# Three mixes in a row: a new order of TensorE's step in a one-core Metaformer kernel, with other banks for the projection and both layers

## The reference

```python
x = x + conv_ref(ln_over_channels(x), w_pc, w_in, fft_w, w_out)
t = to_tokens(x)
t = t + ffn(ln(t), W1, b1, W2, b2)        # products of fp8 (5,2) values, sums kept as fp16
x = from_tokens(t)

def conv_ref(x, w_pc, w_in, fft_w, w_out):
    x = concat([conv3x3(x[:, :12], w_pc), x[:, 12:]])
    x = conv1x1(x, w_in)                  # 48 -> 254 channels
    x = irfft2(rfft2(patches_8x8(x)) * fft_w)
    a, b = split(x, 2)                    # 127 channels each
    return conv1x1(gelu(a) * b, w_out)    # 127 -> 48
```

## Time and profile before

| what | us |
|---|---|
| median of 3 runs (691.2 to 693.7) | 692.02 |
| the profiled execution | 691.75 |
| its span, from the first to the last instruction | 689.9 |
| PE busy | 663.6 |
| DVE busy | 595.6 |
| ACT busy | 534.6 |
| POOL busy | 458.3 |

### The profile page before, as it was taken

One profiled execution on the slowest core, in us unless ns is written; L12 is line 12 of the kernel. 1 busy time (PEld: TensorE's weight loads), 2 busy tenths in 40 slices (PEclk: granted clock), 3 DMA queues, 4 the chain that ended last, 5 costly groups with the idle time before them and its releaser, 6 DMA issues.

```text
span 689.9 us, 19144 instructions
## 1 busy us (share of the span) xinstructions
PE 663.6 (96%) x6604; PEld 525.4 (76%) x6604; DVE 595.6 (86%) x1159; ACT 534.6 (77%) x1086; POOL 458.3 (66%) x348
## 2 busy tenths in 40 slices
PE   6789999999999999999999999999999999999984
PEld 5567787887778878777878787778778877787751
DVE  6668898899988988999889889998988899877887
ACT  3234588988888889888888888888888888777784
POOL 4535667687777777876777778767777787753353
PEclk9999999999999999999999999999999999999995
DMA  4544444554445545544454455445544554342102
GB/s 102 99 112 123 122 103 115 146 141 125 119 118 135 136 114 136 140 128 108 122 141 127 114 143 139 124 107 124 145 118 125 141 141 111 99 123 74 44 24 69
DMA packets 52207, 80.73 MB, mean 117 GB/s; under 512 B 20823, under 2 KB 36079, under 8 KB 52111
## 3 DMA queue, kind: packets, MB, share of 16 engines
q1 hardware_dynamic: 49823, 78.30, 44.2%
q10 hardware_dynamic: 2288, 1.20, 0.7%
HBM read 63.17 MB, written 16.30 MB: 115 GB/s over the span
## 4 chain that ended last, share of the span: by engine, by line
PE 88%; DVE 3%; issue 2%; POOL 2%; DMA 1%; ACT 1%; SPq 1%; DVEq 0%; POOLq 0%; ACTq 0%
PE inva L542 18%; PE invb L549 16%; PE mixp L529 13%; PE misc L558 8%; PE misc L819 8%; PE misc L629 4%; PE misc L529 4%; PE misc L673 3%; PE misc L778 3%; PE misc L578 3%; PE misc L587 2%; PE misc L663 2%; PE mixp L642 2%; PE mixp L649 2%; POOL st L1596 1%
## 5 line engine op out<-in xcount | busy, mean ns | idle before, releaser
L1596 POOL TENSOR_TENSOR st<-st,neg_half 128x16 f32<-128x16 f32 x32 | 92.8, 2901 | 118.6 <-DVE st L1502 118.5
L542 PEld LDWEIGHTS inva<-inv,gmix 128*127 128x127 f32 x1024 | 123.3, 190 | 24.9 <-DVE gmix L1274 12.8
L542 PE MATMUL inva<-inv,gmix 128*127 128x128 f32 x1024 | 141.0, 280 | 0.2 <-DVE gmix L1274 0.2
L1274 DVE TENSOR_TENSOR gmix<-mixp,freq_w 128x508 f32<-128x508 f32 x192 | 122.5, 679 | 15.9 <-PE mixp L529 15.9
L549 PE MATMUL invb<-inv,gmix 128*127 128x128 f32 x1024 | 134.7, 274 | 0.1
L549 PEld LDWEIGHTS invb<-inv,gmix 128*127 128x127 f32 x1024 | 126.1, 191 | 2.1 <-DVE hbuf L1285 0.5
L912 ACT ACTIVATE hid<-misc 128x512 f16<-128x512 f32 x180 | 93.9, 595 | 17.6 <-PE misc L629 17.6
L1630 POOL TENSOR_TENSOR st<-st,neg_half 128x16 f32<-128x16 f32 x31 | 95.5, 3080 | 16.3 <-DVE st L1353 16.3
L1285 DVE TENSOR_TENSOR hbuf<-gact,invb 127x512 f32<-127x512 f32 x128 | 87.3, 682 | 21.3 <-ACT gact L904 16.7
L904 ACT ACTIVATE gact<-inva 127x512 f32<-127x512 f32 x128 | 77.1, 603 | 21.8 <-PE inva L542 21.2
L921 ACT ACTIVATE hid<-hid 128x512 fp8e5<-128x512 f16 x174 | 93.2, 618 | 0.0
(11 more groups left out here) (187 smaller groups left out, 1332.6 us busy)
## 6 DMA issues: line engine op xcount, KB each, us to landing
taps<-cz_scratch SPq DMA_DIRECT2D x63, 292.2 KB
xres<-in_x_dram SPq DMA_DIRECT2D x64, 192.0 KB, 4.3
xin<-in_x_dram SPq DMA_DIRECT2D x63, 192.0 KB, 3.4
out_dram<-ob SPq DMA_DIRECT2D x60, 192.0 KB, 2.6
taps<-cz_scratch SPq DMA_DIRECT2D x63, 146.1 KB
crm<-rm_scratch SPq DMA_DIRECT2D x58, 96.0 KB
cx<-in_x_dram SPq DMA_DIRECT2D x32, 96.0 KB
cz_scratch<-cz SPq DMA_DIRECT2D x63, 48.8 KB
```

The costliest lines, as they stand in the source:

```text
L542: mm = pe.matmul(inva[0:HID, q * PX:(q + 1) * PX], gmix[:, s % 2, q, 0:HID], inv[:], start=True, stop=True, skip_group_check=True)
L1274: dve.tensor_tensor(gmix[:, s % 2, 2 * q:2 * q + 2, 0:HID2], pair[q][:, 0:2 * HID2].rearrange("p (e c) -> p e c", e=2), freq_w[:], ALU.mul ...
L1596: pool.tensor_tensor(st1[:, 6, :], st1[:, 5, :], neg_half[:], ALU.pow).then_inc(pow1, 1)
```

## The change

Mix 2 is written directly behind mixes 0 and 1 and goes to `misc2` and `misc3`; mix 1 stays in `misc0` and `misc1`, mixes 0 and 3 in the `mixp` banks. `gmix` has four slots, so weighing s waits for the inverse s of the band before. The projection goes to the `mixp` banks (before: `misc3` and `misc2`), the second layer to `misc0` and `misc1` (before: `mixp`). The first layer's order is now (0,2), then behind the stream the pair (0,0) and (0,1), mix 3, (1,0), (1,1), `convolve`, and (1,2), written (c,g); each has its bank in a table. From band 3 on the stream uses `misc1` (before: `misc3`). ACT's copies of the first layer follow that order, the last of them in the next step; `order_x` stands ahead of the second layer's copies (`sums`). On DVE weighing 0 stands ahead of the gate 3 of the band before, weighing 2 and gate 0 ahead of the second layer's bias. On SP `rows_in` stands ahead of the store of the output.

The diff, cut to its core:

```diff
-        gmix = sb("gmix", [128, 2, 4, 256])
+        gmix = sb("gmix", [128, 4, 4, 256])
...
+        mix_pair = (mixp, bank[0:2], bank[2:4], mixp)
+        def stream_bank(c):
+            return bank[3 if c < 3 else 1]
+        MADE = {(0, 2): 1, (0, 0): 2, (0, 1): 3, (1, 0): 4, (1, 1): 5, (1, 2): 6}
+        RELUED = {(0, 2): 1, (0, 0): 3, (0, 1): 3, (1, 0): 5, (1, 1): 5, (1, 2): 6}
+        hid_bank = {(0, 2): bank[0], (0, 0): bank[3], (0, 1): bank[2],
+                    (1, 0): bank[0], (1, 1): bank[3], (1, 2): bank[2]}
... (PE, mix and second_layer)
-                pe.wait_ge(gmix_ready, upto(8 * n + 2 * (s if s != 1 else 0)))
-                pair = bank if s == 1 else mixp
+                if s == 0:
+                    pe.wait_ge(gmix_ready, upto(8 * n))
+                pair = mix_pair[s]
...
-                pair = mixp
-                pe.wait_ge(gmix_ready, upto(8 * n + 2, 8 * STEPS))
+                pair = bank
                 pe.wait_ge(hid8_ready, upto(6 * l + 5))
                 pe.sem_inc(pe_held, 1)
                 for c in range(2):
+                    pe.wait_ge(gmix_ready, upto(8 * n + 3 + c, 8 * STEPS))
... (PE, step)
                     mix(t, 1)
+                    pe.wait_ge(hid16_ready, upto(6 * l + 6))
+                    mix(t, 2)
                 if live(t, 4):
-                    pe.wait_ge(lo_ready, upto(2 * n + 1, 2 * STEPS))
-                    project(t, 0, bank[3])
-                    pe.wait_ge(hid16_ready, upto(6 * l + 6))
-                    project(t, 1, bank[2])
+                    pe.wait_ge(gmix_ready, upto(8 * n + 1))
+                    project(t, 0, mixp[0])
+                    pe.wait_ge(gmix_ready, upto(8 * n + 2))
+                    project(t, 1, mixp[1])
...
-                if live(t, 3):
-                    pe.wait_ge(y16_ready, upto(2 * l + 2))
-                    if a >= ROWS_EARLY:
-                        pe.wait_ge(rmT_ready, upto(a + 1, STEPS))
-                    mix(t, 2)
-                if live(t, 5):
-                    pe.wait_ge(q16_ready, upto(2 * k + 2))
...
-                    hidden(t, 0, 0, bank[0])
-                    hidden(t, 0, 1, bank[1])
...
                     if live(t, 5):
-                        pe.wait_ge(tsq_ready, upto(2 * m + 1, 2 * STEPS))
-                        hidden(t, 0, 2, bank[2])
+                        pe.wait_ge(q16_ready, upto(2 * k + 2))
+                        hidden(t, 0, 2, hid_bank[0, 2])
...
+                if live(t, 5):
+                    pe.wait_ge(tsq_ready, upto(2 * m + 2, 2 * STEPS))
+                    hidden(t, 0, 0, hid_bank[0, 0])
+                    hidden(t, 0, 1, hid_bank[0, 1])
                 if live(t, 3):
                     mix(t, 3)
                 if live(t, 5):
+                    pe.wait_ge(hid16_ready, upto(6 * k + 1))
+                    hidden(t, 1, 0, hid_bank[1, 0])
                     pe.wait_ge(hid16_ready, upto(6 * k + 2))
-                    hidden(t, 1, 0, bank[0])
-                    hidden(t, 1, 1, bank[1])
-                    pe.wait_ge(hid16_ready, upto(6 * k + 3))
-                    hidden(t, 1, 2, bank[2])
+                    hidden(t, 1, 1, hid_bank[1, 1])
                 if live(t, 2):
                     convolve(t)
+                if live(t, 5):
+                    pe.wait_ge(hid16_ready, upto(6 * k + 3))
+                    hidden(t, 1, 2, hid_bank[1, 2])
... (ACT, step)
+                if live(t, 6):
+                    accumulator(l, 1, 2)
                 if live(t, 4):
                     gelu(t, 4, 3)
...
-                    accumulators(t, 0, (0,))
...
-                    accumulators(t, 0, (1, 2))
+                    accumulator(k, 0, 2)
                 if live(t, 3):
                     gelu(t, 3, 1)
                 if live(t, 2):
                     ... convs ...
                 if live(t, 5):
-                    accumulators(t, 1, range(3))
+                    accumulator(k, 0, 0)
+                    accumulator(k, 0, 1)
+                    accumulator(k, 1, 0)
                 if live(t, 2):
                     ... zpix ...
+                if live(t, 5):
+                    accumulator(k, 1, 1)
... (DVE, weigh and step)
-                dve.wait_ge(inv_done, upto(8 * n + 2 * s - 2))
+                dve.wait_ge(inv_done, upto(8 * n + 2 * s - 6))
...
+                if live(t, 3) and not first_mix:
+                    weigh(t, 0)
                 if live(t, 4):
                     gate(t, 4, 3)
...
+                if live(t, 3):
+                    weigh(t, 2)
+                    gate(t, 3, 0)
                 if live(t, 6):
                     bias(t)
-                if live(t, 3):
-                    gate(t, 3, 0)
-                if live(t, 3):
-                    weigh(t, 2)
                 if live(t, 4):
                     second_norm(t)
                 if live(t, 5):
-                    relu(t, 0)
+                    relu(k, 0, 2, 1)
                 if live(t, 3):
                     gate(t, 3, 1)
+                if live(t, 5):
+                    relu(k, 0, 0, 2)
```

More of the change, by code:

```diff
@@ L472, in step @@
                     rows_out(t)
+                if live(t, 0) and a > 2:
+                    rows_in(t)
                 if live(t, 6):
@@ L479, in step @@
                           .then_inc(out_stored, 16)
-                if live(t, 0) and a > 2:
-                    rows_in(t)
                 if isinstance(a, int) and a == 2:
@@ L714, in drain @@
                 t = (0, DRAIN)
-                pe.wait_ge(lo_ready, 2 * STEPS)
+                pe.wait_ge(hid16_ready, 6 * OLDER + 5)
                 pe.wait_ge(h_ready, 4 * NEW + 2)
@@ L774, in turn_x @@
                 if FIRST <= t[1] < LAST:
-                    pe.wait_ge(hid16_ready, upto(6 * l + 5))
+                    pe.wait_ge(hid16_ready, upto(6 * l + 4))
                 pe.wait_ge(xord_ready, upto(a + 1))
                 for i in range(PAIRS):
+                    if i == 4 and t[1] > 5:
+                        pe.wait_ge(conv_read, upto(at(t, 3) + 1))
                     mm = pe.transpose(bank[i // 4][:, (i % 4) * 128:(i % 4) * 128 + XSPAN],
@@ L813, in step @@
                         pe.wait_ge(rmT_ready, upto(a))
+                    pe.wait_ge(hid16_ready, upto(6 * l + 5))
                     pe.wait_ge(conv_read, upto(n + 1))
@@ L1308, in rows, with relu @@
                 dve.tensor_tensor(rm[:, 1], order(6), order(2), ALU.mult).then_inc(mr_ready, 1)
-            def relu(t, c, parts=((0, 2), (2, 1))):
-                k = at(t, 5)
-                for g, size in parts:
-                    dve.wait_ge(hid16_ready, upto(6 * k + 3 * c + g + size))
-                    buf = hid16[:, 3 * c + g:3 * c + g + size, :]
-                    dve.tensor_scalar(buf, buf, bq[:, g // 2:g // 2 + 1], 0.0, ALU.add, ALU.max)\
-                       .then_inc(relu_ready, size)
+            def relu(k, c, g, size):
+                dve.wait_ge(hid16_ready, 6 * k + MADE[c, g + size - 1])
+                buf = hid16[:, 3 * c + g:3 * c + g + size, :]
+                dve.tensor_scalar(buf, buf, bq[:, g // 2:g // 2 + 1], 0.0, ALU.add, ALU.max)\
+                   .then_inc(relu_ready, size)
             def scale_tokens(t):
@@ L1481, in step @@
                     low_parts(t, 1)
+                if live(t, 6):
+                    relu(l, 1, 2, 1)
                 if live(t, 0):
@@ L1507, in step @@
                     setup()
-                if live(t, 3) and not first_mix:
-                    weigh(t, 0)
                 if live(t, 3):
```

85 lines of the change are left out of this document (51 added, 34 removed).

## The result

The kernel after takes 705.24 us in the median of 4 runs (702.92 to 707.51), the kernel before 691.62 beside it; the ratio is 1.0191, with a 95% interval of 1.0144 to 1.0237. The forecast was 699.0, between 688.5 and 707.0: slower, as forecast, but by 13.6 us and not by 7. The profiled execution took 706.93 us, with a span of 705.1, against 691.75 and 689.9: 15.2 more.

The account below looks back on a forecast made before the run. PE was taken to bound steps 6 to 31: -0.24 and +0.50 make +0.26 a step, +6.8 us over 26 steps, plus 0.3 elsewhere, giving 699.0 us. Its bounds gave 692 to 705, the stated range 688.5 to 707.0.

Parts of the forecast that it names:

- The seams: PE's switches between full-height fp32 and half-array products, 0.10 each; four move, giving -0.24 us a step.
- The new wait: On PE ahead of (1,1), now in `misc3`: waits for ACT's copy of (0,0), +0.50 us a step.
- The waits with a cover: PE's other waits, as at (0,2), the pair (0,0), (0,1) and (1,0): results come before PE needs them, no cost.
- The rival on DVE: DVE's later bias delays `ob`, the norm and gate 1, making inverse 2's group B late: about 691 us, chance 0.12.
- the long wait: The wait of (1,1) on PE for ACT's copy of (0,0), +0.50 us a step.
- The edges: Steps 3 to 5, the last three and the drain: +0.3 us together, between -1.5 and +2.
- the last rival: Both waits: `ob` also holds back the norm's rest, gate 1 another 0.65 late; +0.61 a step, 708 us, chance 0.12.

Follow-up runs that it names:

- x11: x8 with `convolve` back behind (1,1), POOL's convolved channels earlier, 17 idle products in step 2, (1,1) in `misc1` and `convolve` in `misc3`: 687.38 us.
- x2: The kernel after with ACT copying the stream's result twice, first into a tile nobody reads: 720.62 us, ratio 1.0407.
- x1: The kernel after with PE's `rows` ahead of `turn_tokens` from band 6 on: 701.48 us, ratio 1.0140.
- x12: The kernel after with two banks changed, (1,1) to `misc1` and `convolve` to `misc3`, nothing else: 700.16 us, ratio 1.0124.
- x8: x6 with DVE's square of the first norm's mean ahead of the weighing of mix 0: 694.07 us, ratio 1.0015.
- x6: x4 with `convolve` ahead of (1,0), step 3's weighing 2 and gate 0 ahead of row factors, row factors of steps 3 to 5 in `mixp0`: 695.79 us.
- x4: x1 with DVE's gate 1 behind the second norm's sum of squares instead of the whole norm: 699.02 us, ratio 1.0082.

## Why the forecast was right, and where not

**The seams: right.** -0.24 a step was forecast. When all waits were gone, in x11, the step was 19.55 against 19.78: -0.23. In the kernel after the single prices were `turn_rest` 0.77 (0.78 forecast), inverse 1 group A 0.90 (0.89), the pair 0.23 (0.22).

**The new wait: right in place, cause and size.** ACT's copy of (0,0) ended 5.06 behind `rows` (5.08 forecast), PE was there at 4.66 (4.66), and the wait was 0.45 (0.50, with 0.08 for the start where some 0.05 were needed). x2 shows that ACT's list sets it, x1 that both lists start at `rows`, x12 that the bank is what makes it.

**The waits with a cover: one was missed.** The second layer had been costed as moving at no price. Its new banks wait for DVE's weighing of mix 1: 0.086 a step (x8), 2.2 us in 26 steps. So -0.23 + 0.45 + 0.086 gives 0.30 a step, and 0.26 was forecast; the two errors, 0.05 less and 0.086 more, nearly cancel.

**The rival on DVE: present, behind the long wait.** It was given 0.3 to spare with that wait, and 0.33 were there; without the wait it was to be 0.2 late. In x1 and x12, which leave 0.15 and 0.2 of the wait, that sum would have it 0.05 late and just in time; it was 0.10 and 0.09 late. No run takes the whole wait away with DVE's list as it is. L1370 was held by POOL's `ob` as that rival said, but no more than that.

**The edges: the term that was mis-sized.** +0.3, between -1.5 and +2, was put down for the steps 3 to 5, the last three and the drain. In the profiled execution it is 6.9: step 6 begins 6.8 later. Of that about 2.3 belong to the order at the full clock (x1 against before, from step 3 to step 6: 57.1 and 54.8 us): 1.16 in step 3, for the weighing of mix 2 that stands behind POOL's power; 0.40 in step 4 and 0.76 in step 5. In these two `rows` waits 0.61 each for the copy out of `misc3`, and `turn_rest` 0.90 and 0.53 for the weighing of mix 2, where PE in the kernel before had 0.92 and 0.52 of other idle time; x6, with `rows` in `mixp0`, has step 5 back at 19.75. The forecast had looked at the wait of `rows` in step 5 and not at step 3. The other 4.5 are stretches at 1.2 GHz: 1.7 ahead of step 3, which most kernels with the same set-up don't have, so that the change doesn't explain them, and 2.8 in step 3 (20.05 against 17.27), which come and go between kernels with the same step 3: 1.45 in its forward transform, where the stretch from the set-up goes on, and the rest behind the idle time. The four runs of the kernel after fit: at a mean granted clock of 0.985 and 0.986 they took 702.9 and 703.6 us, at 0.978 (the profiled one) and 0.980 706.9 and 707.5. The single longer steps add 0.5: 26 x 0.30 + 0.5 + 2.3 + 4.5 + 0.1 is 15.2, the difference of the two profiled executions.

**The range: held, in part by luck.** The forecast's own bounds end at 705, and the measured 705.2 lies just above them. The 2 us from there to 707.0 stood for the last rival, in which the rest of the norm is late too, and that did not come; the time of the fill filled them.

What stays open: why PE falls to 1.2 GHz in step 3 in some executions. That its idle time there is the cause fits (four of seven with it, none of five without, and three more falls behind the stream's idle time), but twelve executions are few, the same idle time also passed without a fall in x1, x2 and x4, and no run changes it alone.

## What to carry to other kernels

Price a moved wait by laying the two lists, from the event at which both start to the waiting instruction, side by side: that gave the wait here to 0.05 us. Then ask what stands behind it, for a wait covers others, and taking it away uncovers them (0.45 taken away gave 0.16 in x12); behind the edits of x1, x4 and x8, changing the bank by which a product waits, in place of the order, took the rest (0.16 a step in x11) and made no seam. And go through the steps of the fill one by one, since an order that is free in a full pipeline can wait there for an engine that is late only once.
